# Gated attention with routed experts on one core: probabilities transposed by VectorE and DMA instead of by TensorE

## The chip, the cores and the metric

The kernel runs on one core of a Trainium2 chip. The metric is the device time of one execution in microseconds; each time here is the median of several executions. One more execution was taken by the hardware profiler, and all rows below come from it. The engines are TensorE (PE, with its weight loads PEld), VectorE (DVE), ScalarE (ACT), GpSimd (POOL) and the DMA queue of SyncE (SP).

## What is computed

Eight batches of 512 tokens of width 512. Attention runs in two directions, from `x` to the context and from the context to `x`; a gate mixes the two results; then each token goes to one of eight experts.

```python
Q_char = linear(x_normed, Wq_c, bq_c);  K_sub = linear(ctx, Wk_s, bk_s);  V_sub = linear(ctx, Wv_s, bv_s)
char2sub = softmax(Q_char @ K_sub.T * scale) @ V_sub
Q_sub = linear(ctx, Wq_s, bq_s);  K_char = linear(x_normed, Wk_c, bk_c);  V_char = linear(x_normed, Wv_c, bv_c)
sub2char = softmax(Q_sub @ K_char.T * scale) @ V_char
gate = sigmoid(concat(char2sub, sub2char) @ Wg.T + bg)
x = x + tanh(g_xattn) * (gate * char2sub + (1 - gate) * sub2char)
idx = argmax(softmax(layernorm(x) @ router_w + router_b))
x = x + tanh(g_ffn) * gate_of_expert * (layernorm(x) @ expert_w[idx] + expert_b[idx])
```

## The kernel before

Every matrix product is made in three passes over pairs: each operand is held as a high part in fp32r and the remainder as a low part. Whatever leaves a bank of PSUM for another product is therefore written twice, the high part by ACT, then the low part by DVE. Q and K are folded into one product per direction. A product step on TensorE is 12 matrix multiplications of 128x512.

The order is written out by hand in `steps_of_a_batch`. It is a list of steps (kind, batch offset, direction, tile), and every engine walks the same list and does its own share of each step. The kinds that matter here, each with tiles 0 to 3:

- **Q**: queries; ACT and DVE write `q_pair`. **S**: scores of 128 rows. DVE takes the row maximum (three instructions), ACT the exponential, and DVE then inverts the sum and scales the rows one step later (the last tile's in **NP**).
- **V**: values. **PT**: the probabilities are transposed, four 128x128 blocks on TensorE into the bank `tr0`, and ACT and DVE write the pair `pt_pair`. **U**: attended values, summed in the four banks `u`.
- **KC**: ACT copies the first direction's result from `u` to `kept`. **G**: the gate, two product steps per tile, the first of which reads the first direction's result (`c2s_pair`), the second the second direction's (`q_pair`, written after the last U). **ND**, **XR**: the mix, on DVE.
- **M**, **MX**, **NT**, **NR**, **LG**, **LR**, **RT**, **RK**: transposes, statistics, router and lists of the batch before, spread over this batch.
- **XS**, **XN**, **XD**, **CD**, **CT**, **XA**, **XB**: preparation of the next batch. XS takes a row tile's statistics on DVE, POOL turns them into mean and deviation, XN normalises the tile on ACT, XD reduces it on DVE, CT writes a column tile of the context as a pair (ACT, DVE). When all four tiles have their statistics, SP writes them to DRAM and loads them back spread over all partitions; XA and XB then normalise the transposed `x`, and the next batch's first Q waits for the last XB.

Before the change the order within a batch is Q, S, V with PT and U of the first direction, then the same of the second, then G. Products of Q, V, S and G take the banks `mm0` and `mm1` in turn: each waits until the product before the last has been read. The loop over batches 1 to 6 has one body; batches 0 and 7 stand before and after it.

## Time and profile before

| | us |
|---|---|
| median of 3 runs | 1117.04 |
| range of the runs | 1116.4 to 1117.54 |
| span of the profiled execution | 1115.5 |
| one batch of the loop, from one first G product to the next | 117.0 |

The span runs from the first to the last instruction; 1.5 us of the median lie outside it. TensorE is at its full clock throughout (granted clock 1.000). A line of the timeline gives start, duration, engine, source line, operation and tiles. Matrix multiplications are pipelined, so a duration contains the drain of the last one: the pace of the products is read from one start to the next.

### The profile page before, as it was taken

The numbers are of one execution on the slowest core, as the hardware profiler recorded it, in microseconds if no ns is written. First come the engines' busy times: TensorE is split into PE (matmuls) and PEld (weight loads), VectorE is DVE, ScalarE is ACT, GpSimd is POOL, SyncE is SP. The second block draws the span as 40 slices with busy tenths as digits, with TensorE's granted clock in tenths as the row PEclk, the third lists the DMA queues.
The fourth block names the chain that finished last, engine by engine and source line by source line (L and its number), as shares of the span: only waits on it lengthen the run. The fifth ranks groups of instructions, "written<-read, shape, count | busy, mean of one in ns | idle before, by whom it ended". The sixth has DMA issues, their size and how long they took to land.

```text
span 1115.5 us, 17219 instructions
## 1 busy us (share of the span) xinstructions
...
## 2 busy tenths in 40 slices
...
GB/s 303 114 98 93 123 48 39 46 75 91 75 19 69 122 75 19 69 122 56 19 88 122 38 38 73 113 62 38 50 66 66 114 84 61 222 255 204 188 262 125
DMA packets 71650, 110.04 MB, mean 99 GB/s; under 512 B 24154, under 2 KB 24694, under 8 KB 71608
## 3 DMA queue, kind: packets, MB, share of 16 engines
...
q14 instruction: 20, 0.16, 0.0%
...
## 4 chain that ended last, share of the span: by engine, by line
PE 93%; SPq 2%; issue 2%; DVE 1%; POOL 1%; DMA 1%; ACT 1%; POOLq 0%; DVEq 0%
PE mm L164 60%; PE u L1111 15%; PE u L164 8%; PE tr L1063 4%; PE tr L164 1%; PE mm L1935 1%; PE u L438 1%; PE tr L1155 1%; SPq L1684 1%; DVE arena L1346 1%; SPq L1685 1%; PE mm L484 0%; DMA pairs_as_f<-in_L_ffn_expert_b 0%; DMA slot_as_f<-in_L_ffn_expert_b 0%; SPq L1704 0%
## 5 line engine op out<-in xcount | busy, mean ns | idle before, releaser
L164 PE MATMUL mm<-arena 128*128 128x512 f32 x1512 | 361.8, 392 | 1.6 <-DVE arena L1346 1.6
L164 PEld LDWEIGHTS mm<-arena 128*128 128x128 f32 x1512 | 280.8, 188 | 59.5 <-DVE arena L1346 1.8
L1111 PE MATMUL u<-arena 128*128 128x512 f32 x768 | 188.9, 397 | 0.7 <-DVE arena L1346 0.7
L164 PE MATMUL mm<-arena,q_pair 128*128 128x512 f32 x768 | 180.5, 392 | 0.0
L164 PEld LDWEIGHTS mm<-arena,q_pair 128*128 128x128 f32 x768 | 142.6, 188 | 30.9 <-ACT probs L1217 1.6
L1111 PEld LDWEIGHTS u<-arena 128*128 128x128 f32 x768 | 140.7, 188 | 31.7 <-DVE arena L1346 3.7
L1346 DVE TENSOR_TENSOR arena<-mm,arena 128x512 fp32r<-128x512 f32 x65 | 44.9, 691 | 79.9 <-ACT arena L1212 77.5
L1217 ACT ACTIVATE probs<-mm,neg_top 128x512 f32<-128x512 f32 x64 | 44.1, 689 | 114.2 <-DVE neg_top L1369 114.2
L1208 ACT ACTIVATE q_pair<-mm,c_col 128x512 fp32r<-128x512 f32 x62 | 42.6, 689 | 116.2 <-PE mm L164 113.6
L164 PE MATMUL mm<-c2s_pair,arena 128*128 128x512 f32 x360 | 86.3, 389 | 0.0
L164 PE MATMUL mm<-q_pair,arena 128*128 128x512 f32 x360 | 86.3, 389 | 0.0
L1212 ACT ACTIVATE arena<-mm 128x512 fp32r<-128x512 f32 x64 | 38.1, 595 | 110.1 <-PE mm L164 110.1
L164 PE MATMUL u<-arena,q_pair 128*128 x312 | 77.9, 399 | 3.9 <-DVE q_pair L1896 3.8
L1347 DVE SCALAR_TENSOR_TENSOR q_pair<-mm,c_col,q_pair 128x512 fp32r<-128x512 f32 x62 | 46.4, 750 | 51.2 <-ACT q_pair L1208 50.4
L164 PEld LDWEIGHTS mm<-c2s_pair,arena 128*128 128x128 f32 x360 | 67.6, 188 | 14.0
L164 PEld LDWEIGHTS mm<-q_pair,arena 128*128 128x128 f32 x360 | 67.6, 188 | 14.0
L1554 POOL TENSOR_SCALAR stats<-stats 128x1 f32<-128x1 f32 x32 | 7.6, 238 | 384.8 <-DVE stats L1467 384.5
L164 PEld LDWEIGHTS u<-arena,q_pair 128*128 128x128 f32 x312 | 56.8, 188 | 16.0 <-issue 5.1
L1365 DVE TENSOR_REDUCE mx<-mm 128x1 f32<-128x512 f32 x64 | 44.1, 689 | 38.4 <-PE mm L164 38.4
L1346 DVE TENSOR_TENSOR arena<-tr,arena 128x512 fp32r<-128x512 f32 x67 | 46.1, 688 | 29.2 <-ACT arena L1225 27.7
L1252 ACT ACTIVATE probs<-mm,bg_half 128x512 f32<-128x512 f32 x30 | 20.7, 690 | 100.8 <-PE mm L164 100.8
L1346 DVE TENSOR_TENSOR arena<-slot_as_f,arena 128x512 fp32r<-128x512 f32 x76 | 50.3, 684 | 1.2 <-ACT arena L1266 0.8
...
## 6 DMA issues: line engine op xcount, KB each, us to landing
slot_as_f<-in_x_by_columns SPq DMA_DIRECT2D x14, 1024.0 KB, 8.2
slot_as_f<-in_ctx_by_columns SPq DMA_DIRECT2D x8, 1024.0 KB, 5.8
in_tile<-in_ctx SPq DMA_DIRECT2D x31, 256.0 KB, 2.8
x_rows<-x_tile SPq DMA_DIRECT2D x29, 256.0 KB, 2.1
in_tile<-in_x SPq DMA_DIRECT2D x28, 256.0 KB, 3.0
x_rows_early<-x_tile SPq DMA_DIRECT2D x28, 256.0 KB, 2.3
slot_as_f<-in_L_ffn_expert_w SPq DMA_DIRECT2D x4, 1024.0 KB, 5.7
pairs_as_f<-in_L_ffn_expert_b SPq DMA_DIRECT2D x16, 256.0 KB, 4.5
```

The costliest lines, as they stand in the source:

```text
L164: last = pe.matmul(bank, lhsT(a, c), rhs(b, c), start=start and n == 0, stop=stop and n == C * len(PASSES) - 1)
L438: last = pe.matmul(bank[m][:], pair[0][0][:, a, i, m * P:(m + 1) * P], pair[0][1][:, b, i], start=i == 0 and n == 0, stop=i == C - 1 and n ...
L1063: last = pe.transpose(bank[:, tile(n)], block_of(n), ident[:])
L1111: last = pe.matmul(u_bank[m][:], v_pair[:, i % 2, a, tile(m)], pt_pair[:, i % 2, p], start=i == 0 and n == 0, stop=i == T - 1 and n == 2)
L1155: last = pe.matmul(bank[:, to:to + n * E], part_of_x1t(bb, i, part)[:, tile(t)], router_parts[:, i, 0:n].rearrange("p n e -> p (n e)"), st ...
L1208: act.activation(q_pair[:, HI, i], bank[:], ACT.Identity, bias=c_col[:, d, i:i + 1]).then_inc(q_hi, 1)
L1212: act.activation(v_pair[:, i % 2, HI], bank[:], ACT.Copy).then_inc(v_hi, 1)
L1217: act.activation(probs[:, i], bank[:], ACT.Exp, bias=neg_top[:, d, i:i + 1], scale=SCALE, accum_out=p_sum[:, d, i:i + 1]).then_inc(exp_don ...
L1252: act.activation(probs[:, i], bank[:], ACT.Tanh, bias=bg_half[:, i:i + 1], scale=0.5).then_inc(tanh_done, 1)
L1346: return dve.tensor_tensor(to, bank, f32(hi), ALU.subtract)
L1347: return dve.scalar_tensor_tensor(to, bank, bias, f32(hi), ALU.add, ALU.subtract)
L1365: then(dve.reduce_max(mx[:, d, i:i + 1], bank[:], axis=AX))
```

## The change

- PT leaves TensorE. After a tile's rows are scaled, a new step **PX** lets DVE transpose its 32x32 blocks into a staging buffer. When four are done, SP stores the buffer to DRAM in four DMAs whose runs are 512 bytes long, and loads it back as 128 keys x 4 x 512 queries. PT is now a high part by ACT and a low part by DVE from this SBUF copy.
- Both directions' Q and S come first, then V and U of the first direction, then V and U of the second.
- The result of the first direction is copied from `u` to `kept` at once (KC), and its pair is made from `kept` in a new step **CH**.
- In batch 0 the rows are scaled by DVE in both directions, in place of ACT in the first.
- The previous batch's M, LG, MX, NT, NR and the next batch's XS, XN, XD, CD and CT stand at other places; so do the loads and splits of the expert weights in the last batch (EX).
- Some semaphores are shared.

```diff
-        s = prev("XR", 0) + prev("XR", 1) + cur("Q", 0, 0) + prev("XR", 2) + cur("Q", 0, 1) + prev("XR", 3)
...
-    s += cur("V", 1, 1) + load(10) + late(15) + cur("PT", 1, 1) + table(1) + load(11, 12) + cur("U", 1, 0)
-    s += load(13) + nxt("XD", 1) + nxt("CT", 0) + nxt("XS", 2)
-    s += cur("V", 1, 2) + load(14) + nxt("XN", 2) + cur("PT", 1, 2) + table(2) + load(15) + cur("U", 1, 1) + nxt("CT", 1)
-    s += nxt("XS", 3) + nxt("XD", 2)
-    s += cur("V", 1, 3) + fetch(4, 5) + nxt("XN", 3) + cur("PT", 1, 3) + cur("U", 1, 2)
-    s += nxt("CT", 2) + prev("ID", 0) + nxt("XD", 3)
+        s = steps("""p.XR0 p.XR1 Q00 p.XR2 Q01 p.XR3 Q02 p.NT0 p.M0 p.NT1 Q03 p.NR0 p.MX0
+                     S00 p.NR1 p.LG0 S01 p.M1 S02 PX00 p.LG1 p.MX1 S03 PX01 NP03 PX02
+                     Q10 PX03 p.BS0 p.NT2 p.M2 Q11 p.NR2 p.MX2 p.BS1 p.NT3 Q12 p.M3 p.LG2 p.NR3 p.MX3 Q13 p.LG3 p.LR3""")
+    s += steps("S10") + late(2) + steps("S11 PT00") + late(3) + steps("S12 PX10 PT01 S13 PX11 NP13 PX12")
+    s += steps("V00 PX13 p.BS2 V01 p.BS3 n.CD0 U00") + late(4) + load(0)
+    s += steps("V02 PT02 p.RT0 n.CD1 U01") + late(5) + load(1) + steps("n.XS0 V03 PT03 p.RK0 n.XN0 U02") + late(6)
+    s += load(2, 3) + steps("n.XD0 n.CD2 U03") + late(7) + steps("KC0 KC1 KC2 KC3") + table(0) + steps("V10 PT10") + load(4, 5)
+    s += table(1) + steps("CH0 CH1 V11 PT11") + load(6) + steps("CH2 CH3") + late(8) + table(2) + load(7)
+    s += steps("n.CD3 U10 n.XS1") + late(9) + load(8) + steps("V12 PT12") + load(9)
+    s += steps("n.XN1 n.CT0 U11 n.XD1 n.XS2") + late(10, 11) + load(10, 11) + steps("V13 PT13") + fetch(4, 5)
+    s += steps("n.XN2 n.CT1 U12 n.XD2 n.XS3 n.XN3 n.CT2 p.ID0") + late(12, 13) + load(12, 13, 14)
...
+    s += steps("U13 n.XD3 n.CT3") + late(14, 15) + steps("ND0 ND1 ND2 ND3 n.XA0 n.XA1 n.XA2 n.XA3")
+    return s + steps("G00 n.XB0 n.XB1 G01 n.XB2 n.XB3 G02 G03")
...
+    def turned(d, i):
+        return stage[d].rearrange("p (c t j) -> p c t j", c=blocks, t=T)[:, :, i]
...
+        def store_probs(b, d):
+            await_count(sp, waits_passed_sp, probs_turned, per_dir(b, d, T - 1))
+            for r in range(T):
+                to = pt_dram[d].rearrange("(c i) (r n) -> r i c n", i=32, r=T)[r]
+                sp.dma_start(to, stage[d][32 * r:32 * r + 32].rearrange("i (c n) -> i c n", c=blocks)
+                             ).then_inc(turned_stored, 16)
+        def load_probs(b, d, first=False):
+            await_count(sp, waits_passed_sp, turned_stored, 16 * T * (2 * b + d + 1))
+            if d == 0 and first:
+                sp.wait_ge(x_dotted, T)
+            elif d == 0:
+                await_count(sp, waits_passed_sp, m_tr, 4 * b)
+                await_count(sp, waits_passed_sp, nt_rest, 4 * b)
+            sp.dma_start(by_keys(d), pt_dram[d].rearrange("(c p) q -> p c q", p=P)).then_inc(probs_loaded, 16)
...
-                elif kind == "PT":
-                    if i == 0:
-                        if here == 0 and d == 0:
-                            pe.wait_ge(weights.fold_read, 3)
-                        pe.wait_ge(probs_ready, per_dir(b, d, 3))
-                    transposes(bank, lambda n: probs[:, n, tile(i)]).then_inc(pt_tr, 1)
...
                 elif kind == "PT":
-                    act.wait_ge(pt_tr, per_dir(b, d, i))
-                    act.activation(pt_pair[:, i % 2, HI], bank[:], ACT.Copy).then_inc(pt_hi, 1)
+                    act.wait_ge(probs_loaded, 16 * (2 * b + d + 1))
+                    if i > 1:
+                        act.wait_ge(v_mm, per_dir(b, d, i))
+                    elif d == 1:
+                        act.wait_ge(v_mm, per_dir(b, 1, 0))
+                    act.activation(pt_pair[:, i % 2, HI].rearrange("p (t r j) -> p t r j", t=T, r=T),
+                                   queries_in_order(by_keys(d)[:, i]), ACT.Copy).then_inc(pt_hi, 1)
...
+                elif kind == "PX":
+                    dve.wait_ge(probs_ready, per_dir(b, d, i))
+                    dve.transpose(turned(d, i), probs[:, i].rearrange("p (c j) -> p c j", c=blocks)).then_inc(probs_turned, 1)
...
+                elif kind == "CH":
+                    if i == 0:
+                        dve.wait_ge(turned_stored, 16 * T * (2 * b + 2))
+                    dve.wait_ge(u_hi, per_dir(b, 0, i))
+                    low(c2s_pair[:, LO, i], kept[i], c2s_pair[:, HI, i]).then_inc(u_lo, 1)
```

DVE in the loop, between the scores of tile 2 and of tile 3 of the second direction. `mx` and `neg_top` belong to the row maximum, `p_sum` and `probs` to the scaling of the tile before. Before:

```order
L1365 TENSOR_REDUCE mx<-mm0 128x1
L1329 REGISTER_ALU
L1367 SCALAR_TENSOR_TENSOR mx<-mx,row_const 128x1
L1329 REGISTER_ALU
L1369 TENSOR_TENSOR neg_top<-row_const,mx 128x1
L1340 RECIPROCAL p_sum<-p_sum 128x1
L1329 REGISTER_ALU
L1341 TENSOR_SCALAR probs<-probs,p_sum 128x512
L1365 TENSOR_REDUCE mx<-mm1 128x1
```

Now:

```order
L1361 TENSOR_REDUCE mx<-mm0 128x1
L1328 REGISTER_ALU
L1363 SCALAR_TENSOR_TENSOR mx<-mx,row_const 128x1
L1328 REGISTER_ALU
L1365 TENSOR_TENSOR neg_top<-row_const,mx 128x1
L1336 RECIPROCAL p_sum<-p_sum 128x1
L1328 REGISTER_ALU
L1337 TENSOR_SCALAR probs<-probs,p_sum 128x512
L1373 STREAM_TRANSPOSE pairs_as_f32<-probs 128x16x32
L1342 TENSOR_TENSOR arena<-pairs_as_f32,arena 128x512
L1361 TENSOR_REDUCE mx<-mm1 128x1
```

A block transpose (PX10) and a low part of transposed probabilities (PT01) now stand ahead of the maximum of tile 3.

ACT in the loop, from the high part of the second direction's last V (`arena<-mm1`) to the first read of the finished `u` banks. `in_tile` is XN, `slot3` is CT. Before:

```order
L1212 ACTIVATE arena<-mm1 128x512
L1275 REGISTER_ALU
L1277 ACTIVATE in_tile<-in_tile,mv_x_rest 128x512
L1225 ACTIVATE arena<-tr0 128x512
L1266 ACTIVATE arena<-slot3_as_f32 128x512
L1232 ACTIVATE q_pair<-u0,bv_col 128x512
```

Now:

```order
L1208 ACTIVATE arena<-mm1 128x512
L1223 ACTIVATE arena<-probs 128x512
L1274 REGISTER_ALU
L1276 ACTIVATE in_tile<-in_tile,mv_x_rest 128x512
L1265 ACTIVATE arena<-slot3_as_f32 128x512
L1274 REGISTER_ALU
L1276 ACTIVATE in_tile<-in_tile,mv_x_rest 128x512
L1265 ACTIVATE arena<-slot3_as_f32 128x512
L1228 ACTIVATE q_pair<-u0,bv_col 128x512
```

Two tiles of XN and CT (2 and 3, and 1 and 2) instead of one now stand between the last V and the first `u` bank.

SP in the loop, from the second store of the previous batch's rows on (ISA and REGISTER_ALU are waits). Before:

```order
L888 DMA x1_rows<-x1_tile 128x512
L890 DMA x1_rows_early<-x1_tile 128x512
L173 ISA
L879 ISA
L879 DMA in_tile<-in_ctx_1024 128x512
```

Now:

```order
L868 DMA x1_rows<-x1_tile 128x512
L870 DMA x1_rows_early<-x1_tile 128x512
L174 ISA
L886 DMA probs_by_keys0<-slot8_as_f32 32x16x128 x4
L867 REGISTER_ALU
L868 ISA
L868 DMA x1_rows<-x1_tile 128x512
L870 DMA x1_rows_early<-x1_tile 128x512
L174 ISA
L896 DMA pairs_as_f32<-probs_by_keys0 128x4x512
```

The store of the first direction's probabilities stands before the rows' third store, and the load back after it.

## Rows read from the trace of the kernel before

**Rows 1.** The chain that ended last: its shares of the span by engine.

```profile
PE 93%; SPq 2%; issue 2%; DVE 1%; POOL 1%; DMA 1%; ACT 1%; POOLq 0%; DVEq 0%
```

**Rows 2.** One loop batch: span, busy us (instructions) of PE, PEld, DVE, ACT, POOL; clock.

```profile
365.00:482.00 117.00, 116.93 (x592) 95.95 (x591) 75.45 (x162) 45.03 (x82) 14.09 (x29) 1.00 0.21 68
```

**Rows 3.** Timeline of PE, the same batch: start, us, engine, line, operation, tiles.

```profile
386.72 8.32 PE L164 MATMUL mm<-arena 128*128 128x512 f32 x36
...
429.96 5.72 PE L1111 MATMUL u<-arena 128*128 128x512 f32 x24
435.52 11.04 PE L164 MATMUL mm<-arena 128*128 128x512 f32 x48
446.40 2.88 PE L164 MATMUL mm<-arena,q_pair 128*128 128x512 f32 x12
...
467.13 2.89 PE L164 MATMUL mm<-arena 128*128 128x512 f32 x12
469.86 0.60 PE L1063 MATMUL tr<-ident,probs 128*128 128x128 f32 x4
470.21 3.00 PE L1111 MATMUL u<-arena 128*128 128x512 f32 x12
473.04 2.89 PE L164 MATMUL mm<-arena 128*128 128x512 f32 x12
...
476.12 6.04 PE L1111 MATMUL u<-arena 128*128 128x512 f32 x24
482.00 2.88 PE L164 MATMUL mm<-c2s_pair,arena 128*128 128x512 f32 x12
```

**Rows 4.** Waits: who waited for whom, us in total, times, longest.

```profile
PEld u L1111 <- DVE arena L1346: 3.7, 7, 1.1
```

**Rows 5.** Instruction groups: busy us, mean ns of one, idle before.

```profile
L1346 DVE TENSOR_TENSOR arena<-slot_as_f,arena 128x512 fp32r<-128x512 f32 x76 | 50.3, 684 | 1.2 <-ACT arena L1266 0.8
L1341 DVE TENSOR_SCALAR probs<-probs,p_sum 128x512 f32<-128x512 f32 x60 | 29.2, 487 | 2.1
```

**Rows 6.** Timeline, DVE, then ACT, around one tile of scores.

```profile
455.30 0.69 DVE L1365 TENSOR_REDUCE mx<-mm 128x1 f32<-128x512 f32 x1 [0.45 <-PE mm L164]
...
456.22 0.16 DVE L1369 TENSOR_TENSOR neg_top<-row_const,mx 128x1 f32<-128x1 f32 x1
...
456.49 0.49 DVE L1341 TENSOR_SCALAR probs<-probs,p_sum 128x512 f32<-128x512 f32 x1
```

**Rows 7.** Timeline of ACT: exponential, XN of tiles 2 and 3, first read of `u`.

```profile
456.41 0.69 ACT L1217 ACTIVATE probs<-mm,neg_top 128x512 f32<-128x512 f32 x1 [1.44 <-DVE neg_top L1369]
...
471.37 0.82 ACT L1277 ACTIVATE in_tile<-in_tile,mv_x_rest 128x512 f32<-128x512 f32 x1 [0.72 <-POOL mv_x_rest L1556]
...
477.06 0.82 ACT L1277 ACTIVATE in_tile<-in_tile,mv_x_rest 128x512 f32<-128x512 f32 x1 [0.49 <-POOL mv_x_rest L1556]
...
480.13 2.07 ACT L1232 ACTIVATE q_pair<-u,bv_col 128x512 fp32r<-128x512 f32 x3 [1.26 <-PE u L1111]
```

**Rows 8.** Timeline of DVE: XA begins, XB ends, XS of tiles 2 and 3 end.

```profile
371.29 0.69 DVE L1403 TENSOR_TENSOR slot_as_f<-slot_as_f 128x512 f32<-128x512 f32 x1 [1.41 <-DMA slot_as_f<-x_row_statistics]
...
380.46 1.29 DVE L1346 TENSOR_TENSOR arena<-slot_as_f,arena 128x512 fp32r<-128x512 f32 x2
...
469.51 0.18 DVE L1422 BATCH_NORM_AGGREGATE mv_x_rest<-bn_x 128x2 f32<-128x6 f32 x1 [0.15 <-DVE bn_x L1421]
...
474.75 0.18 DVE L1422 BATCH_NORM_AGGREGATE mv_x_rest<-bn_x 128x2 f32<-128x6 f32 x1 [0.15 <-DVE bn_x L1421]
```

**Rows 9.** Timeline of SP: the statistics of the next batch are stored.

```profile
477.26 0.41 SPq L960 DMA_DIRECT2D x_row_statistics<-mv_x  x1
```

**Rows 10.** DMA issues: out<-in, queue, count, KB each, median us to landing.

```profile
slot_as_f<-in_x_by_columns SPq DMA_DIRECT2D x14, 1024.0 KB, 8.2
slot_as_f<-in_ctx_by_columns SPq DMA_DIRECT2D x8, 1024.0 KB, 5.8
...
x_rows<-x_tile SPq DMA_DIRECT2D x29, 256.0 KB, 2.1
...
x_rows<-stats SPq DMA_DIRECT2D x8, 32.0 KB, 1.8
```

More of the change, by code:

```diff
@@ L491, in weights_part @@
     part.first_stats = first_stats
+    part.dve_links, part.links, part.pool_chain, part.pool_done = dve_links, links, pool_chain, pool_done
     return part
 def steps_of_a_batch(first, last):
-    def one(kind, rel, d, i):
-        return [(kind, rel, d, i)]
-    cur = lambda kind, d, i: one(kind, 0, d, i)
-    prev = (lambda kind, i: one(kind, -1, 0, i)) if not first else (lambda kind, i: [])
-    nxt = (lambda kind, i: one(kind, 1, 0, i)) if not last else (lambda kind, i: [])
-    late = (lambda *ns: [("WT", 0, 0, n) for n in ns]) if first else (lambda *ns: [])
@@ L517, in steps_of_a_batch, with steps @@
-    load = (lambda *ks: [("EX", 0, 0, n) for n in ks]) if last else (lambda *ks: [])
+    late = lambda *ns: [("WT", 0, 0, n) for n in ns] if first else []
+    load = lambda *ks: [("EX", 0, 0, n) for n in ks] if last else []
+    fetch = lambda *ks: [("EL", 0, 0, n) for n in ks] if last else []
+    table = lambda i: [("TB", 0, 0, i)] if last else []
+    def steps(names):
+        out = []
+        for name in names.split():
+            rel = {"p": -1, "n": 1}.get(name[0] if "." in name else "", 0)
+            kind, _, d, i = step_of(name[2:] if rel else name)
+            if (rel >= 0 or not first) and (rel <= 0 or not last):
+                out.append((kind, rel, d, i))
+        return out
@@ L519, in steps_of_a_batch @@
     if first:
-        names = """W11 FR0 SM0 W12 W13 Q00 Q01 FOLD0 Q02 Q03 SC00 SC01 SC02 SC03 A10 SC10 WT0 A11 SC11 SC12 FOLD1 SC13
-                   CT0 A12 CT1 CT2 A13 CT3 WT1 XD0 FOLD2 AH10 AH11 AL10 S00
-                   XD1 AL11 WH2 S01 XD2 WL2 WH3 S02 XD3 WL3 S03 NP03"""
-        s = [step_of(name) for name in names.split()]
-    else:
-        s = prev("XR", 0) + prev("XR", 1) + cur("Q", 0, 0) + prev("XR", 2) + cur("Q", 0, 1) + prev("XR", 3)
-        s += cur("Q", 0, 2) + prev("M", 0) + prev("M", 1) + prev("MX", 0) + prev("MX", 1) + prev("NT", 0) + prev("BS", 0)
-        s += cur("Q", 0, 3) + prev("NT", 1) + prev("M", 2)
-        s += cur("S", 0, 0) + prev("BS", 1) + prev("NR", 0) + cur("S", 0, 1) + prev("MX", 2)
-        s += cur("S", 0, 2) + prev("NR", 1) + cur("S", 0, 3) + prev("M", 3) + cur("NP", 0, 3)
@@ L560, in steps_of_a_batch @@
-    s += cur("U", 1, 3) + nxt("CT", 3)
-    for i in range(C):
-        s += cur("ND", 0, i)
-    for i in range(C):
-        s += nxt("XA", i)
-    return (s + cur("G", 0, 0) + nxt("XB", 0) + nxt("XB", 1) + cur("G", 0, 1) + nxt("XB", 2) + nxt("XB", 3)
-            + cur("G", 0, 2) + cur("G", 0, 3))
-def steps_of_the_last_gate(cur, load):
-    gather = lambda *ns: [("GA", 0, 0, n) for n in ns]
-    s = gather(0, 1, 2) + load(16, 17) + cur("U", 1, 3) + [("EL", 0, 0, 6)] + load(18, 19)
-    s += cur("GC", 0, 0) + load(20, 21) + cur("ND", 0, 0) + cur("ND", 0, 1)
-    s += cur("GC", 0, 1) + load(22, 23) + cur("ND", 0, 2) + cur("ND", 0, 3)
-    s += cur("GC", 0, 2) + load(24, 25) + cur("GC", 0, 3) + load(26, 27) + [("EL", 0, 0, 7)] + gather(3, 4)
-    s += cur("GS", 0, 0) + [("TN", 0, 0, 0)] + load(28) + cur("GS", 0, 1) + load(29, 30)
-    return s + cur("GS", 0, 2) + load(31) + [("TP", 0, 0, 0)] + cur("GS", 0, 3)
+        s = steps("""W11 FR0 SM0 W12 W13 Q00 Q01 FOLD0 Q02 Q03 SC00 SC01 SC02 SC03 A10 SC10 A11 SC11 SC12 FOLD1 SC13
+                     CT0 A12 CT1 CT2 A13 CT3 XD0 FOLD2 AH10 AH11 AL10 S00
+                     XD1 AL11 AH12 S01 XD2 AL12 AH13 S02 XD3 AL13 PX00 S03 PX01 NP03 PX02
+                     Q10 PX03 CD0 CD1 Q11 CD2 SR0 Q12 CD3""") + late(0, 1) + steps("Q13")
+    else:
+        s = steps("""p.XR0 p.XR1 Q00 p.XR2 Q01 p.XR3 Q02 p.NT0 p.M0 p.NT1 Q03 p.NR0 p.MX0
+                     S00 p.NR1 p.LG0 S01 p.M1 S02 PX00 p.LG1 p.MX1 S03 PX01 NP03 PX02
+                     Q10 PX03 p.BS0 p.NT2 p.M2 Q11 p.NR2 p.MX2 p.BS1 p.NT3 Q12 p.M3 p.LG2 p.NR3 p.MX3 Q13 p.LG3 p.LR3""")
@@ L1147, in run @@
                 elif kind == "LG":
-                    bank = take(b, step, here) if i == 0 else tr_bank_of(step)
+                    bank = take(b, step, here) if i == 0 else tr_bank_of(step, bb)
                     pe.wait_ge(nt_third, per_batch(bb, i))
@@ L1202, in run @@
                 bb = b + rel
-                bank = banks.take((kind, rel, d, i))
+                bank = banks.take((kind, rel, d, i), bb)
                 if kind == "Q":
@@ L1351, in run @@
                 bb = b + rel
[L1352 removed]
+                bank = banks.take((kind, rel, d, i), bb)
                 if kind == "Q":
@@ L1600, in gpsimd @@
         lists_filled()
-        done = chain["n"]
+        done = chain["base"] + chain["n"]
         chain.update(n=0)
```

190 lines of the change are left out of this document (91 added, 99 removed).

## The prediction

> **What bounds the kernel now.** I read the chain first. PE holds 93% of it [rows 1], so a change gains only what it takes from PE's own time, and loses whatever it makes PE wait. Then one loop batch: PE is busy for 116.93 of 117.00 us, DVE for 75.45, ACT for 45.03 [rows 2]. So PE has no idle time to give; DVE has some 41 us a batch. Then the pace on PE [rows 3]: four product steps from 435.52 to 446.40 are 2.72 each, and 40 steps in a batch make 108.8. The other 8.2 us are the small steps between products, and waits. A transposed tile costs twice: 0.35 itself (469.86 to 470.21), and the product behind it starts its successor 2.83 later (470.21 to 473.04), 0.11 more than the pace.
>
> **What PE no longer does.** Eight PT steps a batch at 0.35: 2.8 us. The interruptions fall from 12 to 8, by the order of PE's instructions, since M and LG stay and some PTs stood next to them: 4 x 0.11 = 0.44. Two small waits around the PTs, about 0.2 each, go with them (estimated from the remainder of the sum). One more goes: the last two U steps of the second direction take 5.88 (476.12 to 482.00), those of the first 5.56 (429.96 to 435.52), 0.32 more, and the trace has PE's loads waiting there for the low part of PT, seven times, 3.7 us in all [rows 3, 4]. Behind V13, PT13 now stands directly, with XN3 moved away. Sum: about 4.0 us a batch, 32 over eight; without any new wait the time would be 1085.
>
> **The block transposes on DVE.** The trace has none. Its nearest rows: a scaled row tile takes 0.49, a low part from SBUF 0.68 [rows 5]; twice that, 1.37, is my upper bound for an instruction that reorders. I take 0.68 (one element per partition and cycle, like the low part), and 0.61 back to back, since queued instructions overlap their starts by 0.08. Eight are 5 us a batch, which DVE's 41 us hold on average. What counts is where PE waits next, the scores of the second direction. I count from the end of S03 on PE. M, LG and four Q put the ends of S10 to S13 at 15.3, 18.0, 20.8, 23.5. A tile's maximum starts 0.1 after its end and the negated top is there 1.1 later (455.30 to 456.38); the exponential ends 0.7 after that (456.41 to 457.10) [rows 6, 7]. DVE: S11 to 19.2, scaling to 19.8; ACT's PT00 20.1 to 20.7; PT00 low 20.8 to 21.4; S12 to 22.4 (exponential 23.3; V00 needs it at 23.5, just in time); scaling 23.0, PX10 23.7, PT01 low 24.8 behind ACT's high part; S13 to 25.8, exponential 26.8. V01 takes the same bank and could start at 26.2: **0.65 a batch** lost. At 1.37 a transpose V01 loses 0.6 more and U00 some 0.8, since V00's low part falls behind. The same sum for the first direction, with M and LG between its scores, gives no wait.
>
> The Trainium skill has two statements here. "VectorE: DVE Perf Modes", section "The three transpose paths", has 311 ns for a 128x128 block in bf16, four of which would be 1.24 us. "Vector Engine (DVE) Microarchitecture Reference", section 3.8, says one element per cycle per lane, which is the value taken. No row here decides it; by the first the batch would lose what the upper bound loses.
>
> **The trip through DRAM.** PX03 ends at 5.1 on that clock, so SP issues the four stores from 5.3. The load waits for them and for M3 and NT3 (both about 9.6). ACT's PT00 stands ahead of the exponential of S12, so a late load holds S12, then V00. ACT can start PT00 by 20.1 without loss. A 1 MB load lands 5.8 after its issue, 8.2 beside other traffic [rows 10], so it must be issued by 14.3: the stores have 9 us from their first issue. 256 KB stored in 128 runs take 2.1, 512 runs of 64 bytes 1.8 [rows 10]; four of either, in sequence, give 7.2 to 8.4, overlapped less. I take no loss, and a bound of 8 us more for the stores. The other direction has twice the time: stores from about 30, PT10 wanted near 50. What is queued behind the waits on SP: the third and fourth store of rows, two context tiles, the context's columns. Each is wanted over 10 us later, so I cost that at nothing.
>
> **KC and CH.** The same eight evictions and eight low parts as before in number. KC follows each bank's last product, V10 and V11 give PE 5.4 us to hide it, and CH is read by G 20 us later: no cost.
>
> **The preparation of the next batch.** This is the term that eats the gain. Now the clock starts at the end of U03. PE goes V10 2.7, V11 5.4, U10 8.2, V12 10.9, U11 13.6, V13 16.3, U12 19.0, U13 21.8. From the end of XS to the start of XN, through POOL, it is 1.7 (469.69 to 471.37) to 2.1 (474.93 to 477.06) [rows 7, 8]. DVE: CD3 after CH3 to 9.5, XS1 to 10.8; XN1 12.5 to 13.3, CT0 low to 14.6; XD1 15.3; XS2 16.7; V13 and PT13 low to 18.4. XN2 18.4 to 19.2, CT1 low 20.5, XD2 21.2, XS3 22.6. XN3 24.3 to 25.1, CT2 high 25.7, and only then ACT reads `u0` for the pair of the second direction: 26.3, low part 27.1. G's first product ends at 24.5 and the next reads that pair: **2.6 us** lost a batch. In the profile XN3 starts at 477.06 and ACT waits for the first bank at 480.13 [rows 7]: there that work was done before U13 ended. The second path says the same: the statistics' store went out at 477.26, XA began 11.0 later (371.29 a batch on), and XB ended 10.46 after XA began (371.29 to 381.75) [rows 8, 9]. Now the store goes out at 24.5, XB ends at 46.0. PE ends G at 21.8 + 8 x 2.72 + 2.6 = 46.1, and Q00 of the next batch needs the last XB: no further loss, but a shorter wait at G would gain nothing either. Before, XB ended 5 us ahead of Q00 (386.72) [rows 3].
>
> **Sum.** A loop batch: -4.0 + 0.65 + 2.6 = -0.75, six of them -4.5. Batch 0: eight PTs and the wait for the first, -4.7; +0.65, +2.6 and about 0.8 for DVE, which now also scales rows beside the start's splits: -0.65. Batch 7 prepares no next one: -3.9 + 0.65 = -3.25. The experts' part is untouched. Together -8.4 on the 1115.5 of the profiled span, 1107.1, and with the 1.5 outside the span **1108.6** against the median of 1117.04. With the bounds of the transposes and waits in it the case runs from 1102 to 1114.
>
> **The rivals.**
> - *The preparation is not late* (XS1 gets its turn earlier than I count, or POOL's 1.7 overlaps). Both paths, 7 x 2.6, go: 1090, down to 1085. For it: DVE idles in my timetable before XS2. Against: four tiles in a row, each with a trip DVE, POOL, ACT, DVE.
> - *The transposes take 1.37.* 1.4 more a batch, 8 times: 1108.6 + 11 = 1120, and the stores start 2.4 later.
> - *The stores are slow* (the other side). One mechanism: the load lands after 20.1, ACT sits at PT00, the exponential of S12 waits behind it, and PE waits at V00. Every us past the 9 costs 8 us in total; it decides against the change from just over 10 us for the four stores. At 14 it is 5 a batch: 1108.6 + 40 = 1149. For it: 2048 runs of 512 bytes from 32 partitions at a time, a pattern that no row shows, with two stores of rows close behind in the queue. Against: 512 runs of 64 bytes landed in 1.8 [rows 10].
>
> The skill's section "The three transpose paths" warns that a plain DMA whose access pattern does the transposing is 19 times slower than the hardware's transposing DMA when the innermost stride is large. Here the blocks are transposed already and the runs are contiguous, so I don't take it to apply; if it did, it would be the last rival at its worst.
>
> **How the numbers follow.** Forecast 0.47, preparation not late 0.20, transposes at the bound 0.13, stores slow 0.20. The measurement can tell about 0.2% (2.2 us) from no change. Below 1114.8 lie the second case and most of the first: 0.62. Within 2.2 us of 1117.04 lie the edge of the forecast, half of the transposes' case: 0.12. Slower: the slow stores and the rest: 0.26. The range of 8 in 10 leaves out the far end of the slow stores and the very best: 1087 to 1132. The likeliest case's own range is 1102 to 1114.
>
> **What would show it.** PE's row of probabilities transposed is gone; its products keep 2.72. The block transpose has its own row: 0.6 to 0.7. V01 starts late by about 0.6. G00's second product waits 2 to 3 us for a low part of `q_pair`, and ACT reads `u0` after XN3. The load of the first direction's probabilities lands before PT00 is wanted. The pitch of a batch is 116.3. I am wrong if PE waits at V00 for ACT (stores), at U00 for V00's low part (transposes), or nowhere (113).

## The result, and the profile after

| | before | after |
|---|---|---|
| median, us | 1116.93 | 1120.99 |
| range of four runs each, us | 1116.4 to 1117.54 | 1119.28 to 1124.81 |
| span of the profiled execution, us | 1115.5 | 1117.5 |
| pitch of a loop batch, us | 117.04 | 116.05 |

The kernel became slower by 0.4%: ratio 1.0041, interval 1.0023 to 1.0059. The forecast was 1108.6, so its sign was wrong. Yet a loop batch did become shorter, by 1.0 where 0.75 was forecast.

The chain that ended last no longer runs through PE alone (93% in [rows 1]):

```profile
PE 72%; DVE 11%; issue 6%; ACT 5%; POOL 3%; SPq 2%; DMA 1%; POOLq 0%; DVEq 0%; ACTq 0%
```

**A loop batch.** First one batch from G00 to G00 (columns as in [rows 2]), then what PE waited for in the whole kernel:

```profile
370.55:486.60 116.05, 113.60 (x560) 92.67 (x559) 79.41 (x170) 44.55 (x81) 15.43 (x29) 1.00 0.35 105
```

```profile
PE mm L165 <- DVE q_pair L1343: 14.1, 6, 2.4
PE mm L165 <- issue: 11.2, 1, 11.2
```

PE's busy time fell by 3.3 us a batch (116.93 to 113.60), and 2.4 of it came back as one wait, six times. Its place in the timeline of PE, at the second product of G00:

```profile
375.78 3.02 PE L165 MATMUL mm<-q_pair,arena 128*128 128x512 f32 x12 [2.35 <-DVE q_pair L1343]
378.64 2.89 PE L165 MATMUL mm<-c2s_pair,arena 128*128 128x512 f32 x12
```

and ACT, which must write the high part first:

```profile
372.94 0.81 ACT L1276 ACTIVATE in_tile<-in_tile,mv_x_rest 128x512 f32<-128x512 f32 x1 [4.14 <-POOL mv_x_rest L1560]
373.66 0.61 ACT L1265 ACTIVATE arena<-slot_as_f 128x512 fp32r<-128x512 f32 x1
374.18 2.40 ACT L1228 ACTIVATE q_pair<-u,bv_col 128x512 fp32r<-128x512 f32 x4
```

U13 ended near 370.7, but ACT stood at XN3 until 372.94 and read `u0` at 374.18. In [rows 7] XN3 started at 477.06, ahead of U13's end.

**Batch 0.** This is the row that no step of the prediction has. Timeline of PE around the first G of batch 0:

```profile
125.25 3.06 PE L1111 MATMUL u<-arena 128*128 128x512 f32 x12 [0.42 <-DVE arena L1342]
139.48 4.52 PE L165 MATMUL mm<-c2s_pair,arena 128*128 128x512 f32 x12 [11.18 <-issue]
143.83 2.91 PE L165 MATMUL mm<-q_pair,arena 128*128 128x512 f32 x12
146.58 2.88 PE L165 MATMUL mm<-c2s_pair,arena 128*128 128x512 f32 x12
```

U13 is done at 128.3, earlier than before; then PE does nothing for 11.2 us. Before, the same products stood at 130.79, 133.51 and 136.23. A wait put down to "issue" has no releaser in the profile, so it is read from the code: in batch 0 the first G waits for all sixteen splits of late-loaded weights (`pe.wait_ge(wt_lo, 4 * C)`). The last ones, WT14 and WT15, stand behind U13, XD3 and CT3, and these behind XN3 and CT2, which wait for POOL. ACT (`slot_as_f` at L1272 is a split), then the last lows on DVE:

```profile
130.82 0.81 ACT L1276 ACTIVATE in_tile<-in_tile,mv_x_rest 128x512 f32<-128x512 f32 x1 [4.12 <-POOL mv_x_rest L1560]
131.53 0.61 ACT L1265 ACTIVATE arena<-slot_as_f 128x512 fp32r<-128x512 f32 x1
132.05 1.13 ACT L1272 ACTIVATE arena<-slot_as_f 128x512 fp32r<-128x512 f32 x2
133.09 2.40 ACT L1228 ACTIVATE q_pair<-u,bv_col 128x512 fp32r<-128x512 f32 x4
135.37 0.64 ACT L1265 ACTIVATE arena<-slot_as_f 128x512 fp32r<-128x512 f32 x1
135.89 1.15 ACT L1272 ACTIVATE arena<-slot_as_f 128x512 fp32r<-128x512 f32 x2
```

```profile
137.48 1.90 DVE L1342 TENSOR_TENSOR arena<-slot_as_f,arena 128x512 fp32r<-128x512 f32 x3
```

The three lows end at 139.38 and PE starts at 139.48. The next product starts 4.35 later and not 2.72: the granted clock (the third number from the end of each line) had fallen while PE was idle:

```profile
128.00:140.00 12.00, 0.82 (x3) 0.50 (x2) 8.68 (x18) 6.23 (x11) 1.05 (x3) 0.69 0.41 105
140.00:144.00 4.00, 4.00 (x13) 3.16 (x12) 3.27 (x6) 0.00 (x0) 0.00 (x0) 0.66 0.96 288
144.00:148.00 4.00, 4.00 (x19) 3.27 (x19) 3.90 (x7) 1.22 (x3) 0.00 (x0) 1.00 0.66 255
```

It was 1.00 up to 131, and 0.50, the lower of its two levels, from 134 to 140; the values in between are means of stretches that hold both.

**The account** of the two profiled spans. The third G product: 136.23 before, 146.58 after, +10.35 (8.69 of it the later start, 1.6 the clock). From there to the first gate product of batch 7: 813.80 before (136.23 to 950.03), 804.59 after (146.58 to 951.17), -9.2. The rest: 165.5 and 166.3, +0.9. Together +2.0, as the spans say. The medians differ by 4.1: the profiled run of after is the quickest of its four, and its mean clock is 0.995, that of the other three 0.988 to 0.990. Where the other three lost their clock no trace shows.

### The profile page after: what moved, and what is told of

Same layout as the page of the kernel before. It is cut to its first block, busy times and chain, and to the rows that moved or that the text cites. A ratio compares the mean times of both kernels' runs of the same rounds, so it can differ in the third digit from the quotient of the medians.

```text
span 1117.5 us, 16995 instructions
## 1 busy us (share of the span) xinstructions
PE 1071.7 (96%) x5247; PEld 872.6 (78%) x5247; DVE 776.7 (70%) x1614; ACT 447.2 (40%) x804; POOL 207.6 (19%) x325
## 4 chain that ended last, share of the span: by engine, by line
PE 72%; DVE 11%; issue 6%; ACT 5%; POOL 3%; SPq 2%; DMA 1%; POOLq 0%; DVEq 0%; ACTq 0%
PE mm L165 49%; PE u L1111 8%; PE u L165 7%; DVE arena L1342 3%; DVE mx L1361 2%; ACT probs L1215 2%; PE tr L165 1%; PE tr L1071 1%; DVE bn_x L1425 1%; PE u L437 1%; ACT arena L1265 1%; PE mm L1937 1%; DVE junk L1442 1%; DVE c2s_pair L1342 1%; PE tr L1155 1%
## 5 line engine op out<-in xcount | busy, mean ns | idle before, releaser
L1111 PE MATMUL u<-arena 128*128 128x512 f32 x768 | 183.2, 390 | 1.8 <-DVE arena L1342 1.6
L165 PE MATMUL mm<-arena,q_pair 128*128 128x512 f32 x768 | 184.1, 394 | 0.0
L1111 PEld LDWEIGHTS u<-arena 128*128 128x128 f32 x768 | 143.4, 188 | 32.4 <-DVE arena L1342 3.0
L1558 POOL TENSOR_SCALAR stats<-stats 128x1 f32<-128x1 f32 x32 | 13.9, 434 | 514.0 <-DVE stats L1471 513.8
L165 PE MATMUL mm<-c2s_pair,arena 128*128 128x512 f32 x360 | 88.0, 394 | 11.2 <-issue 11.2
L165 PEld LDWEIGHTS mm<-c2s_pair,arena 128*128 128x128 f32 x360 | 68.6, 191 | 26.0 <-issue 11.6
L1768 POOL DMA_INDIRECT out<-slot_as_f,u_row x39 | 41.0, 1052 | 40.1 <-DVE slot_as_f L1913 28.1
L1251 ACT ACTIVATE probs<-mm,bg_half 128x512 f32<-128x512 f32 x30 | 20.5, 684 | 63.6 <-PE mm L165 63.6
```

The costliest lines, as they stand in the source:

```text
L165: last = pe.matmul(bank, lhsT(a, c), rhs(b, c), start=start and n == 0, stop=stop and n == C * len(PASSES) - 1)
L1111: last = pe.matmul(u_bank[m][:], v_pair[:, i % 2, a, tile(m)], pt_pair[:, i % 2, p], start=i == 0 and n == 0, stop=i == T - 1 and n == 2)
L1251: act.activation(probs[:, i], bank[:], ACT.Tanh, bias=bg_half[:, i:i + 1], scale=0.5).then_inc(tanh_done, 1)
L1558: then(pool.tensor_scalar(rstd, var, EPS, None, ALU.add))
L1768: pool.indirect_dma_start(out=out_rows, out_offset=bass.IndirectOffsetOnAxis(ap=idx[:, n:n + 1], axis=0), in_=y[n % OUT], in_offset=None, ...
```

## The experiments

**Theory A:** the loss lies in batch 0, at one wait of PE behind a queue. **Theory B:** it is spread over the batches, in the wait at G and in DVE's heavier load. All times are medians of 4 or 5 runs beside runs of the kernel before on the same chip; ratios are to it. The changed kernel was not run again beside them. The kernel before took 1116.3 to 1117.0 there, and 1122.5 in one case named below, so a difference to the changed kernel is known to about 1 us.

### The splits ahead of the chain

```diff
-... late(10, 11) + load(10, 11) + steps("V13 PT13") + fetch(4, 5)
-    s += steps("n.XN2 n.CT1 U12 n.XD2 n.XS3 n.XN3 n.CT2 p.ID0") + late(12, 13) + ...
-    s += steps("U13 n.XD3 n.CT3") + late(14, 15) + steps("ND0 ...
+... late(10, 11) + load(10, 11) + steps("V13 PT13") + late(12, 13) + fetch(4, 5)
+    s += steps("n.XN2 n.CT1 U12 n.XD2 n.XS3") + late(14, 15) + steps("n.XN3 n.CT2 p.ID0") + ...
+    s += steps("U13 n.XD3 n.CT3") + steps("ND0 ...
```

> The changed kernel; only batch 0's four last splits of the gate weights (WT12 to WT15) stand earlier on ACT and DVE: 12 and 13 right behind PT13, 14 and 15 behind XS3, ahead of XN3 and CT2, where the trace has both engines idle for 1 to 4 us. Theory A (the loss lies in batch 0, where PE's first G product waits for all sixteen splits): PE's idle 11.2 us before the first G product of batch 0 falls to 2 to 3, the clock stays at 1.00 through that batch, and the median falls from 1121.0 by 8 to 11, to 1110 to 1113; the pitch of a loop batch stays 116.05. Theory B (the loss is in every batch: the wait for the pair of the second direction and DVE's heavier load): less than 2 us of change, 1119 or more.

Measured: **1110.81**, ratio 0.9948 (0.9931 to 0.9964), 10.2 below the changed kernel. The place of four splits, in one batch, is worth more than the whole loss of 4.1. PE at the same place, then the clock there:

```profile
131.53 5.46 PE L165 MATMUL mm<-c2s_pair,arena 128*128 128x512 f32 x12 [2.83 <-issue]
136.78 3.35 PE L165 MATMUL mm<-q_pair,arena 128*128 128x512 f32 x12
```

```profile
131.00:137.00 6.00, 5.47 (x13) 4.35 (x14) 3.70 (x7) 4.15 (x7) 1.03 (x2) 0.50 0.29 50
```

The idle time fell from 11.2 to 2.8, the start by 7.95. The expectation that the clock stays at 1.00 was wrong: behind 2.83 us of idle it was 0.50, and the next product started after 5.25. The start at 131.53 is again just behind the last lows of the splits, which end on DVE at 131.42.

### The fills of the lists earlier

In batch 0 ACT stands before KC0 (and with it PT10) for a list fill to land:

```profile
106.61 0.69 ACT L1246 ACTIVATE normed<-u,bv_col 128x512 f32<-128x512 f32 x1 [5.17 <-DMA token_lists<-x_tile]
```

```diff
-                    if 2 <= i < 2 + FILLS:
-                        fill_lists(i - 2)
+                    if i < FILLS:
+                        fill_lists(i)
...
                     if i == 0:
...
-                            lists_filled()
                             act.wait_ge(weights.router_split, 2 * PARTS - 1)
                     if i == T - 1:
+                        if first:
+                            lists_filled()
```

> The changed kernel; in batch 0 ACT issues the five fills of the token lists at WT0 to WT4 instead of WT2 to WT6, and waits for them ahead of the last copy KC3 (whose buffer they read) instead of KC0. Theory A: the 5.2 us that ACT stands ahead of KC0 go, the steps behind come 2 to 5 us earlier, and the splits WT14 and WT15 with them: 1116 to 1119. If the splits are held by the chain of row statistics alone, not by this wait, the gain is under 1 us. Theory B: no change, 1120 to 1122.

> Both edits of the two runs before. Theory A: both waits of batch 0 are gone; with the first G product then set by PE's own order, at some 2 us less than with the splits alone: 1108 to 1111, which is the 1108.6 that was forecast without these waits. Theory B: 1119 or more.

Measured: **1123.64** alone, ratio 1.0054 (1.0033 to 1.0075), and **1111.92** with the splits ahead, 0.9958 (0.9941 to 0.9975), 1.1 above the splits alone. The intervals overlap in both pairs, so neither difference is shown; the gain of 2 to 5 us that was expected if the wait holds the splits did not come. The 5 us wait went, but the chain of statistics sets WT14, and PE still stood 11.2 ahead of G. Two fills were now issued at 67.23, between the stores of the probabilities (64.34 in both kernels) and the load back, which went out at 72.90 instead of 70.96. ACT's PT00 started at 77.68 in the changed kernel; here:

```profile
79.28 0.63 ACT L1223 ACTIVATE arena<-pairs_as_f 128x512 fp32r<-128x512 f32 x1 [1.48 <-DMA pairs_as_f<-probs_by_keys]
```

and PE waits 2.29 where it had waited 0.63:

```profile
83.16 7.38 PE L165 MATMUL mm<-arena 128*128 128x512 f32 x24 [2.29 <-ACT probs L1215]
```

### The chain of the next batch earlier

```diff
-    s += table(1) + steps("CH0 CH1 V11 PT11") + load(6) + steps("CH2 CH3") + ...
-    s += steps("n.CD3 U10 n.XS1") + ... + steps("V12 PT12") + load(9)
-    s += steps("n.XN1 n.CT0 U11 n.XD1 n.XS2") + ... + steps("V13 PT13") + ...
-    s += steps("n.XN2 n.CT1 U12 n.XD2 n.XS3") + late(14, 15) + steps("n.XN3 n.CT2 p.ID0") + ...
+    s += table(1) + steps("n.CD3 n.XS1 V11 PT11") + load(6) + steps("CH0 CH1") + ...
+    s += steps("n.XN1 U10 n.XD1 n.XS2") + ... + steps("V12 PT12") + load(9)
+    s += steps("CH2 n.XN2 CH3 U11 n.XD2 n.XS3") + ... + steps("V13 PT13") + ...
+    s += steps("n.XN3 n.CT0 U12 n.XD3 n.CT1") + late(14, 15) + steps("p.ID0") + ...
...
+    s += steps("U13 n.CT2 n.CT3") + steps("ND0 ...
```

> As the run before, and in every batch the chain of the next batch's row statistics stands earlier: CD3 and XS1 ahead of CH0, XN1 ahead of U10, XN2 ahead of U11, XN3 ahead of U12; CT0 to CT3 follow the tiles' chain instead of standing in it. If the preparation of the next batch is what holds PE at G (the step of the prediction that gave 2.6 us a batch), the wait for the pair of the second direction goes from 2.4 us to under 0.5 and the last XB ends several us before Q00: the pitch falls from 116.05 to 113.5 to 114.3, and the time to 1092 to 1098. If it is not that, or if the earlier steps make PE wait for V and PT low parts on DVE instead, the pitch stays within 0.7 of 116.05: 1107 to 1112.

Measured: **1100.36**, ratio 0.9854 (0.9838 to 0.9871), pitch 114.15 (249.48 to 363.63). The pitch is as expected, the time 2.4 above the range. Beside e3_both, which it extends, that is 11.6 less. So Theory B was half right: the wait at G, which was forecast, is worth more than the loss of 4.1 too, as the splits are, which were not. The early chain with the splits left in their late place was not run. The wait at G is gone; 0.5 of it is left at U13:

```profile
360.76 3.03 PE L1111 MATMUL u<-arena 128*128 128x512 f32 x12 [0.52 <-DVE arena L1343]
363.63 2.65 PE L165 MATMUL mm<-c2s_pair,arena 128*128 128x512 f32 x11
```

### Only U13 ahead of XN3

```diff
-    s += steps("n.XN2 n.CT1 U12 n.XD2 n.XS3") + late(14, 15) + steps("n.XN3 n.CT2 p.ID0") + ...
-    s += steps("U13 n.XD3 n.CT3") + steps("ND0 ...
+    s += steps("n.XN2 n.CT1 U12 n.XD2 n.XS3") + late(14, 15) + steps("p.ID0") + ...
+    s += steps("U13 n.XN3 n.CT2 n.XD3 n.CT3") + steps("ND0 ...
```

> As e1_splits_ahead; in every batch U13 stands ahead of XN3 and CT2 of the next batch, so that ACT reads the finished u banks first. The prediction's two paths: if the second one (the statistics' store, then XA and XB, which Q00 of the next batch needs) is as late as the first, the wait for the pair of the second direction at G goes (2.4 us to under 0.3) and comes back as a wait of about the same length at Q00: 1109 to 1113, the pitch 115.7 to 116.5. If only the first path counts: 2.4 us a batch less, 1093 to 1097.

Measured: **1109.99**, ratio 0.9940 (0.9923 to 0.9956), 0.8 below the splits alone. PE (`probs` at L1251 is the gate's tanh, which frees a bank):

```profile
379.84 3.04 PE L165 MATMUL mm<-c2s_pair,arena 128*128 128x512 f32 x12 [1.25 <-ACT probs L1251]
386.31 8.46 PE L165 MATMUL mm<-arena 128*128 128x512 f32 x36 [0.71 <-DVE arena L1342]
```

Of the 2.35 us, 1.96 came back, 0.71 at Q00 for the last XB and 1.25 at G02 for a bank, which ACT frees between its steps XB. The pitch varies from 115.3 to 116.5 over the batches, beside 115.96 to 117.64 in e1_splits_ahead. The prediction's second path is real: to read the banks earlier gains next to nothing while the chain behind them is as late.

### The price of PE's transposes, in the kernel before

These two kernels leave the transposes of the probabilities out.

```diff
                 elif kind == "PT":
...
-                    transposes(bank, lambda n: probs[:, n, tile(i)]).then_inc(pt_tr, 1)
...
-                    act.activation(pt_pair[:, i % 2, HI], bank[:], ACT.Copy).then_inc(pt_hi, 1)
+                    act.activation(pt_pair[:, i % 2, HI], probs[:, i], ACT.Copy).then_inc(pt_hi, 1)
```

> The kernel before, with the transposes of the probabilities left out on PE; ACT and DVE read the untransposed probabilities from SBUF in their place, so the attended values are not the reference's. It prices what the change takes from PE. The prediction's first term (4.0 us a batch, 32 in all): 1083 to 1088. If PE's transposes cost only what stands in their own rows (0.35 each, 2.8 a batch): 1093 to 1096. If they hid behind waits that stay: above 1100.

Measured: **1110.63**, ratio 0.9941 (0.9924 to 0.9957): the third of the expectations, above 1100, by which the transposes hid behind waits that stay. Of 32 us only 6.3 came. PE, and ACT ahead of it:

```profile
360.73 3.01 PE L1110 MATMUL u<-arena 128*128 128x512 f32 x12 [2.05 <-DVE arena L1349]
```

```profile
358.62 0.81 ACT L1280 ACTIVATE in_tile<-in_tile,mv_x_rest 128x512 f32<-128x512 f32 x1 [2.02 <-POOL mv_x_rest L1559]
359.34 0.61 ACT L1228 ACTIVATE arena<-probs 128x512 fp32r<-128x512 f32 x1
```

PT13's high part stands behind XN3, which waits for POOL: the same chain, in the kernel before. PE's transposes had covered it. So XN2 and XN3 were moved behind PT12 and PT13:

```diff
-    s += cur("V", 1, 2) + load(14) + nxt("XN", 2) + cur("PT", 1, 2) + ...
+    s += cur("V", 1, 2) + load(14) + cur("PT", 1, 2) + nxt("XN", 2) + ...
...
-    s += cur("V", 1, 3) + fetch(4, 5) + nxt("XN", 3) + cur("PT", 1, 3) + cur("U", 1, 2)
+    s += cur("V", 1, 3) + fetch(4, 5) + cur("PT", 1, 3) + nxt("XN", 3) + cur("U", 1, 2)
```

> As e6_no_pe_transpose (the kernel before without PE's transposes of probabilities, so the attended values are not the reference's); the normalisation steps XN2 and XN3 of the next batch stand behind PT12 and PT13 instead of ahead of them on ACT. In e6 PE waits 2.05 us a batch at U13 and 0.35 at U10 for the low part of PT, which stands behind XN3 and XN1. If that wait alone hid the price of PE's transposes: the pitch falls from 116.1 to 113.5 to 114.1, and the time to 1092 to 1097. If the chain of the next batch then holds PE at G or at Q00 instead: 1107 or more.

Measured: **1090.53**, ratio 0.9766 (0.9751 to 0.9781), pitch 113.78 (240.70 to 354.48). That is 1.5 below the range expected, with the pitch inside it. In this order of steps the transposes are worth 117.04 - 113.78 = 3.26 a batch and 25.9 in all. A wait of 0.34 at U10 is left: V10 and V11 take 6.23 from start to start there, where two products take 5.44.

### The cause put into the kernel before

```diff
-    ... cur("V", 1, 0) + late(13, 14)
+    ... cur("V", 1, 0) + late(13)
...
-    s += cur("V", 1, 1) + load(10) + late(15) + cur("PT", 1, 1) + ...
-    s += cur("U", 1, 3) + nxt("CT", 3)
+    s += cur("V", 1, 1) + load(10) + cur("PT", 1, 1) + ...
+    s += cur("U", 1, 3) + nxt("CT", 3) + late(14, 15)
```

> The kernel before, with only one edit: in batch 0 the splits WT14 and WT15 stand behind U13 and CT3 instead of at V10 and V11. Theory A: PE's first G product, which needs all sixteen, then waits 4 to 6 us behind CT3's low part and two more low parts, and the clock falls behind the idle time: 1121 to 1125, spread above 2 us. Theory B (the batch-0 order was no part of the loss): 1115.5 to 1117.5.

Measured: **1120.91**, ratio 1.0034 (1.0020 to 1.0048). Two splits in another place cost the kernel before 3.9 us, as much as the whole change did:

```profile
133.27 4.58 PE L164 MATMUL mm<-c2s_pair,arena 128*128 128x512 f32 x12 [3.41 <-issue]
137.69 2.89 PE L164 MATMUL mm<-q_pair,arena 128*128 128x512 f32 x12
```

The start is 2.5 later than before (130.79), and the clock costs 1.7 more (4.42 to the next product against 2.72): 4.2, measured 3.9. The wait at 3.4 was shorter than the 4 to 6 expected.

### The chain early and the splits spread

The order of e4_chain_early, without the earlier fills of the lists, with XD2 behind PT13 and with the splits of batch 0 spread from U00 on.

```diff
+    s += steps("V00 PX13 p.BS2 V01 p.BS3 n.CD0 U00") + late(4, 5) + load(0)
+    s += steps("V02 PT02 p.RT0 n.CD1 U01") + late(6, 7) + ... + steps("n.XS0 V03 PT03 p.RK0 n.XN0 U02") + late(8, 9)
+    s += load(2, 3) + steps("n.XD0 n.CD2 U03 KC0 KC1 KC2 KC3") + late(10, 11) + ...
...
+    s += steps("CH2 n.XN2 CH3 U11 n.XS3") + late(13) + load(10, 11) + steps("V13 PT13 n.XD2") + late(14) + ...
```

> The early chain of e4_chain_early without the earlier fills, with the splits of batch 0 spread from U00 on two by two, and with XD2 behind PT13, so that the low part of PT13 is ready for U13. If the 0.5 us wait at U13 of each batch, the 1.65 at U13 and the 2.4 before G of batch 0 are what is left of the reordering, 1094 to 1098; if the earlier splits only make other waits in batch 0, 1098 to 1101.

Measured: **1088.38**, ratio 0.9745 (0.9729 to 0.9762), 32.6 below the changed kernel and 6 under the range expected. Pitch 113.33 (241.07 to 354.40), with no wait at U13, G or Q00; and in batch 0 the 1.25 us of idle time no longer cost clock (2.84 to the next product):

```profile
127.59 3.00 PE L165 MATMUL mm<-c2s_pair,arena 128*128 128x512 f32 x12 [1.25 <-issue]
130.43 2.88 PE L165 MATMUL mm<-q_pair,arena 128*128 128x512 f32 x12
```

Against the early chain with the earlier fills (1100.36) that is 12.0: 6.0 at the start of the first G (133.57 to 127.59), 1.6 of clock there (4.40 to the next product against 2.84), 0.82 in each of six batches.

### The row maximum first

```diff
-    ... + steps("S12 PX10 PT01 S13 PX11 NP13 PX12")
-    s += steps("V00 PX13 p.BS2 V01 ...
+    ... + steps("S12 S13 PX10 PT01 PX11 NP13")
+    s += steps("V00 PX12 PX13 p.BS2 V01 ...
```

> As e8_chain_and_splits; in every batch the block transposes of tiles 0 and 2 of the second direction (PX10, PX12) and the low part of PT01 stand behind the row maximum of tile 3, which then starts when its scores end. The prediction gave the lateness of V01 behind them 0.65 us a batch. If that holds: 5 us less, 1083 to 1085, pitch 112.7. If V00's low part, now the last of a row of five DVE steps, holds U00 instead: no gain, 1087.5 to 1089.

> e8_chain_and_splits in batch 0, e9_row_maximum_first in batches 1 to 7. The pitch in e9 was 112.96 against 113.33 in e8, and its batch 0 had a wait of 1.2 us at U13 that e8 had not. If both hold: 7 x 0.37 = 2.6 below e8's 1088.4, 1085 to 1086.5, with a spread under 2 us. If the wait of batch 0 comes from the opening and not from the order: no better than e9, 1087 or more.

The second of them has this order in batches 1 to 7 only. Measured: **1087.24**, ratio 0.9733 (0.9719 to 0.9747), and 0.9756 (0.9739 to 0.9773) for the second, which ran on a chip where the kernel before took 1122.46 and it 1095.4. As totals both are inconclusive against 0.9745, and the first hits neither of its two expectations. The profiles are clearer: the pitch fell from 113.33 to 112.96 and 112.98, so V01's wait was worth 0.37 a batch. In the first a wait of 1.2 at U13 of batch 0 took part of it back. In the second the first gate product of batch 7 starts 2.25 earlier than in e8_chain_and_splits (918.78 against 921.03), of the 2.6 expected, while the experts' part behind it is 9 us longer (175.1 against 166.0 to the end of the span), on a chip where before was 6 us longer too.

### Every block transpose twice

```diff
                 elif kind == "PX":
                     dve.wait_ge(probs_ready, per_dir(b, d, i))
+                    then(dve.transpose(turned(d, i), probs[:, i].rearrange("p (c j) -> p c j", c=blocks)))
                     dve.transpose(turned(d, i), probs[:, i].rearrange("p (c j) -> p c j", c=blocks)).then_inc(probs_turned, 1)
```

> The changed kernel with every block transpose done twice on DVE, so that a step PX takes about 1.5 us instead of 0.65 (0.70 for the extra one and about 0.15 until DVE may go on). Theory A (DVE's load as such is not the loss; only the step before the scores of tile 3 counts): the prediction's bound of 1.4 us a batch, 8 to 12 us more in all, 1128 to 1133, with all of it at V01 and U00 of each batch. Theory B (DVE's load is what made the kernel slower): every one of the eight extra 0.85 us a batch shows, over 40 us more, 1160 or above.

Measured: **1159.65**, ratio 1.0394 (1.0378 to 1.0410), 38.7 above the changed kernel: Theory A's size for this edit was wrong, and Theory B's nearly right. The pitch is 122.00, +5.95. Cut at the starts on PE, against the same stretches of the changed kernel: from S10 to G00 56.75 against 55.42, **+1.3**, the 1.4 that the prediction had for V01 and U00. From Q10 to S10 +1.4, where PE's transposes M3 wait for a bank:

```profile
444.63 0.66 PE L1071 MATMUL tr<-ident,pairs_as_f 128*128 128x128 f32 x4 [1.11 <-ACT x_tile L1285]
```

From G00 to Q00 +1.6, the clock: behind the same wait of 2.35 at G the granted clock was 0.61 on average in this profile (388.4 to 392.8; 4.46 to the next start) and 1.00 in that of the changed kernel (2.86). From Q00 to S00 +1.8, which is not the transposes' time at all:

```profile
414.19 1.42 DVE L1463 SCALAR_TENSOR_TENSOR pairs_as_f<-probs,tanh_g,slot_as_f 128x512 f32<-128x512 f32 x2 [2.67 <-issue]
```

This is the first step of the loop's body on DVE (XR0), with no wait of its own left. And this queue of instructions has 46 packets, where every other kernel here has 20:

```profile
q14 instruction: 46, 0.38, 0.1%
```

Read together: with eight more instructions and their waits the body of DVE's loop seems to be fetched anew at each turn. That is an inference from two rows; a body of the same length without the work was not run. So this kernel does not price DVE's load cleanly. Against DVE's load as the cause of the loss stand the splits (10.2 us from their place alone) and e8_chain_and_splits, which does all of DVE's work of the changed kernel in 1088.

## Why the prediction was wrong

**The step that failed** is in the sum: "Batch 0: eight PTs and the wait for the first, -4.7; +0.65, +2.6 and about 0.8 for DVE, which now also scales rows beside the start's splits: -0.65." Measured, G's third product of batch 0 starts 10.35 us later than before, where this step has it 0.65 earlier. These 11.0 us are more than the 10.4 between the span forecast (1107.1) and the span profiled (1117.5). The gain up to U13 was there: it ended at 131.0 before, at 128.3 after. What the step lacks is PE's wait for the sixteen splits. WT14 and WT15 moved from behind V10 and V11 to behind U13 and CT3, and the prediction counted XN3, CT2 and the `u` banks in exactly that row of ACT, in every batch, and never asked what else stood in it in the first one. Of a step that is moved, who waits for it must be asked in every batch in which it exists. The clock made it 1.6 more, which no step had.

**PE's transposes, -4.0 a batch.** Right. Beside the 108.8 of the 40 products the pitch held 8.2 before. In the changed kernel it holds 7.25; of these 2.65 are the wait at G (378.64 - 370.55 for two products, less 5.44) and 0.39 the one at V01, so 4.2 is left, and 4.0 was taken away. The two kernels without either wait have a pitch of 112.96 and 112.98, 4.1 below 117.04. "Without any new wait the time would be 1085" stands beside 1087.24 (e9_row_maximum_first), which still waits 1.2 at U13 of batch 0. The 3.26 of e11_no_pe_transpose_xn is the price in the old order of steps, with the wait at U10 left in it.

What the prediction did not see is that in the kernel before, too, the next batch's chain through POOL and ACT lay just under the transposes: their removal alone is worth 6.3 us there (2.05 of wait at U13). [rows 7] showed ACT waiting 0.72 and 0.49 for POOL ahead of PT12 and PT13.

**The block transposes at 0.68.** Right; the bound of 1.37 was too high by half. Groups on DVE, busy us, mean ns:

```profile
L1373 DVE STREAM_TRANSPOSE slot_as_f<-probs 128x512 f32<-128x512 f32 x32 | 22.5, 704 | 0.0
L1373 DVE STREAM_TRANSPOSE pairs_as_f<-probs 128x512 f32<-128x512 f32 x32 | 22.4, 701 | 0.0
```

0.70 us for 128x512, as much as the low part of the same size takes (0.69 in the changed kernel). That decides between the two readings of the Trainium skill that the prediction weighed: the trace agrees with one element per cycle per lane ("Vector Engine (DVE) Microarchitecture Reference", section 3.8) in that the transpose has the pace of an ordinary pass. The 1.24 was an estimate, four times the 311 ns that "VectorE: DVE Perf Modes", section "The three transpose paths", has for one 128x128 block in bf16; no run here has such a block alone, and 128x512 in one instruction did not cost four times that.

**V01, +0.65 a batch.** Mechanism right, size 0.37. PE's two V products took 5.83 from start to start where two take 5.44:

```profile
326.17 5.99 PE L165 MATMUL mm<-arena 128*128 128x512 f32 x24
332.00 2.88 PE L1111 MATMUL u<-arena 128*128 128x512 f32 x12
```

The price set on slower transposes was right as well: with every transpose done twice, V01 and U00 lose 1.3 more (e10_transposes_twice), where 1.4 was said.

**The trip through DRAM, no loss.** Right. DMA issues, KB each, us to landing:

```profile
probs_by_keys<-slot_as_f SPq DMA_DIRECT2D x32, 256.0 KB, 4.0
pairs_as_f<-probs_by_keys SPq DMA_DIRECT2D x8, 1024.0 KB, 6.0
```

A store takes 4.0, twice what the nearest rows said, but the four overlap: in that batch they were issued from 307.73, the load at 315.06, 7.3 later, inside the 9 us allowed (12.4 on the prediction's clock, where 14.3 was the latest). PT00 on ACT had no wait (first of the two lines is the exponential of S11):

```profile
322.10 0.69 ACT L1215 ACTIVATE probs<-mm,neg_top 128x512 f32<-128x512 f32 x1 [1.94 <-DVE neg_top L1365]
322.78 0.62 ACT L1223 ACTIVATE arena<-pairs_as_f 128x512 fp32r<-128x512 f32 x1
```

In batch 0 the cover is thin: with the fills earlier (e2_lists_early) PE waited 1.7 us longer for it (2.29 against 0.63).

**The preparation of the next batch, +2.6 at G, nothing at Q00.** Right: 2.35, and XB ended as Q00 was due. DVE begins XA at 384.36, PE's Q00 follows G without a gap at 394.96 (24.4 us after G00 started, which is 46.2 on the prediction's clock, where it said 46.1):

```profile
384.36 0.69 DVE L1407 TENSOR_TENSOR slot_as_f<-slot_as_f 128x512 f32<-128x512 f32 x1 [2.62 <-DMA slot_as_f<-x_row_statistics]
```

"A shorter wait at G would gain nothing either": e5_u13_first.

**KC and CH.** No cost in the loop, as said. In batch 0 KC0 carries the wait for the lists, 5.2 us of ACT, which held PE 1.22 at U10. Its removal gained nothing.

**The sum.** A loop batch was forecast as -4.0 + 0.65 + 2.6 and measured as -4.1 + 0.4 + 2.65. From G's third product of batch 0 to batch 7 the forecast was -7.75 and the trace has -9.2. With the splits ahead the kernel takes 1110.8, against the 1108.6 forecast. **The rivals:** "the preparation is not late" (1090) is what e8_chain_and_splits made of it, 1088.4. "The transposes take 1.37" was priced at 1.4 a batch at V01 and U00; that much came there when they took twice as long, and 1.4 more at M3, so 1120 was too low a price for it.
